# One Trainium2 kernel: the down products of the last group moved behind its gate and up products

## What is computed

```
for t in range(32):                                    # cell(h, x_t)
    r = sigmoid(x W_ih_r + h W_hh_r + b);  z = sigmoid(...)
    n = tanh(x W_ih_n + b + r * (h W_hh_n + b));  h = (1 - z) * n + z * h
gu = h @ wq_gu.T                 # 256 -> 2048, ternary weights by groups of 64
gate, up = split(gu)             # 1024 each
hid = silu(gate) * up
hn  = hid * rsqrt(mean(hid * hid) + eps)               # mean over the 1024 hidden values
out = x + hn @ wq_p.T            # 1024 -> 256
```

## Time and profile before

| | |
|---|---|
| median of 3 runs | 346.22 us (346.09 to 346.31) |
| the profiled execution | 346.3 us, of which the span of the profile is 344.5 us |
| PE busy | 339.4 us (99% of the span) |
| DVE, ACT, POOL busy | 233.6, 222.8, 184.0 us |
| granted PE clock | 1.00 of full speed |

### The profile page before, as it was taken

The page is one execution under the profiler, slowest core; times in us unless marked ns, Lnnn a source line. Parts: engine busy times, 40 slices in busy tenths (PEclk is TensorE's granted clock), DMA queues, the critical chain, the costliest instruction groups (busy, mean ns, idle before and its releaser), DMA issues.

```text
span 344.5 us, 5631 instructions
## 1 busy us (share of the span) xinstructions
PE 339.4 (99%) x2059; PEld 295.2 (86%) x2059; DVE 233.6 (68%) x462; ACT 222.8 (65%) x438; POOL 184.0 (53%) x156
## 2 busy tenths in 40 slices
PE   8999999999999999999999999999999999999996
PEld 4889988788988889888888889888888888888895
DVE  7578788899677565755667554875558555664866
ACT  5768888886756757555766656566564655756662
POOL 2315571465825446255454446444472554799694
PEclk9999999999999999999999999999999999999999
DMA  7994000045001000140001000010000100010101
GB/s 240 319 410 192 3 0 2 0 148 220 1 2 62 2 0 0 44 142 2 0 0 63 0 2 0 2 63 0 2 0 2 60 1 2 0 64 1 57 6 61
DMA packets 7891, 18.72 MB, mean 54 GB/s; under 512 B 564, under 2 KB 4788, under 8 KB 7352
## 3 DMA queue, kind: packets, MB, share of 16 engines
q1 hardware_dynamic: 7176, 17.97, 13.9%
q10 hardware_dynamic: 688, 0.39, 0.4%
HBM read 14.17 MB, written 4.19 MB: 53 GB/s over the span
## 4 chain that ended last, share of the span: by engine, by line
PE 94%; DVE 3%; ACT 1%; issue 1%; DVEq 0%
PE ps_ffn L1105 30%; PE ps_out L1143 16%; PE ps_rz L1017 7%; PE ps_rz L1022 7%; PE ps_rz L1018 7%; PE ps_n L1017 3%; PE ps_n L1022 3%; PE ps_n L1018 3%; PE ps_rz L1105 2%; PE ps_ffn L1270 2%; PE ps_t L1098 1%; PE ps_ffn L1017 1%; PE ps_ffn L1022 1%; PE ps_ffn L1018 1%; PE ps_n L1055 1%
## 5 line engine op out<-in xcount | busy, mean ns | idle before, releaser
L354 POOL TENSOR_TENSOR hid_lo<-work,hid_hi 128x512 fp32r<-128x512 f32 x62 | 81.7, 1317 | 103.6 <-ACT hid_hi L452 99.6
L1105 PE MATMUL ps_ffn<-st_hi,wguT 128*128 128x512 f32 x236 | 93.7, 397 | 0.3 <-DVE work L737 0.3
L1105 PE MATMUL ps_ffn<-st_lo,wguT 128*128 128x512 f32 x236 | 92.7, 393 | 0.0
L361 POOL TENSOR_TENSOR sq_sum<-sq_sum,work 128x512 f32<-128x512 f32 x55 | 73.2, 1331 | 1.8 <-ACT work L466 0.6
L737 DVE TENSOR_TENSOR work<-work,ps_ffn 128x512 f32<-128x512 f32 x55 | 37.6, 683 | 31.5 <-ACT work L448 31.5
L452 ACT CAST hid_hi<-work 128x512 fp32r<-128x512 f32 x63 | 38.8, 616 | 23.0 <-DVE work L747 23.0
L1105 PEld LDWEIGHTS ps_ffn<-st_hi,wguT 128*128 128x128 f32 x236 | 44.4, 188 | 8.3 <-DVE work L737 0.9
L1105 PEld LDWEIGHTS ps_ffn<-st_lo,wguT 128*128 128x128 f32 x236 | 44.5, 189 | 7.3
L747 DVE TENSOR_TENSOR work<-work,ps_ffn 128x512 f32<-128x512 f32 x63 | 43.2, 686 | 4.7 <-PE ps_ffn L1105 2.8
L1143 PEld LDWEIGHTS ps_out<-wpT,hid_hi 128*128 128x128 f32 x240 | 35.8, 189 | 3.7
L1143 PE MATMUL ps_out<-wpT,hid_lo 128*128 128x256 f32 x240 | 38.8, 284 | 0.0
(11 more groups left out here) (226 smaller groups left out, 716.0 us busy)
## 6 DMA issues: line engine op xcount, KB each, us to landing
out_dram<-o_st SPq DMA_DIRECT2D x7, 512.0 KB, 2.6
xT_all<-in_x_dram SPq DMA_DIRECT2D x1, 3072.0 KB, 17.6
x_ring<-in_x_dram SPq DMA_DIRECT2D x1, 3072.0 KB, 11.5
x_ring<-in_L_ffn_w_gate_up_dram SPq DMA_DIRECT2D x4, 512.0 KB, 8.9
x_ring<-in_L_ffn_w_proj_dram SPq DMA_DIRECT2D x2, 512.0 KB, 11.6
x_ring<-in_x_dram SPq DMA_DIRECT2D x1, 1024.0 KB, 5.4
work<-in_L_cond_W_ih_dram SPq DMA_DIRECT2D x3, 256.0 KB, 4.4
work<-in_L_cond_W_hh_dram SPq DMA_DIRECT2D x3, 256.0 KB, 4.6
```

What stands on the lines that cost most here:

```text
L354: nc.gpsimd.tensor_tensor(hid_lo[:, j % RING], hid[:, j % 2], f32(hid_hi[:, j % RING]), ALU.subtract).then_inc(hid_lo_ok, 1)
L361: nc.gpsimd.tensor_tensor(sq_sum[:], sq_sum[:], hid_sq[:, j % 2], ALU.add).then_inc(sq_added, 1)
L1105: mm = pe.matmul(bank, w, group_state(part, G, k), start=(k == 0 and i == 0), stop=(k == KD - 1 and i == 1))
```

## The change

In the last group (G = 7):

- `PE_END` now ends with all gate and up products, of tile 7 too, whole and not in halves. Down products of tiles 0 to 2 stay among them (items "E0" to "E2", in a different order of steps for tile 0). Behind "U7" come: the high parts of tiles 3 to 7, the low part of tile 3, the squares once for all eight tiles, the low parts of tiles 4 to 6, and the low part of tile 7 step by step, each step with its own signal.
- POOL computes the low parts of tiles 0 to 2 alone, and adds the squares of tiles 1 to 7. DVE computes the low parts of tiles 3 to 7: that of tile 3 behind `hidden` of tile 5, that of tile 4 behind `hidden` of tile 6, those of 5, 6 and (behind the mean) 7 at the end.
- `hid`, its high and its low parts of this group go to eight places each, in buffers that are no longer needed (`xT_all`, `wi_hi`, `wi_lo`, `wh_hi`, `wh_lo`, `hid_lo`), so `hidden` no longer waits for them. The four steps' outputs go to four banks (`ps_out` twice, `ps_n`, `ps_t`).
- The mean is made once, the power -1/2 still in two halves, and `rows_out` waits for each step's signal. The first two steps' store is now two stores.
- In all groups the square waits for `hid_ok` itself as well.

```diff
-          "U5", "D3", "G6", "U6", "D4", "Ga", "Ua", "Gb", "Ub", "D5", "H6", "T0", "T2", "Ta", "Tb", "L0", "L2"]
+          "U5", "G6", "U6", "G7", "U7"]
...
+        def hid_of(G, j):
+            return late[:, j] if is_late(G) else hid[:, j % 2]
...
+        last_out = (ps_out[:, 0, :], ps_out[:, 2, :], ps_n[:, 0:D], ps_t[:, 0:D])
+        last_sq = gate_bank(NG - 1, HT - 2)[:, 0:GS]
+        POOL_LOWS, DVE_LOWS = (0, 1, 2), (3, 4, 5, 6, 7)
...
+            for j in range(1, HT):
+                if j in POOL_LOWS:
+                    low_part(G, j)
+                add_square(G, j)
+            pool.wait_ge(ms_ok, NG)
...
-            hidden_hi(G, 5)
-            silu_part(G, 6)
-            hidden_square(G, 5)
-            hidden_hi(G, 6)
-            last_silu("a")
-            hidden_square(G, 6)
-            last_silu("b")
-            last_hi("a")
-            last_square("a")
-            last_square("b")
-            last_hi("b")
+            hidden_square(G, HT - 1)
+            hidden_hi(G, HT - 1)
...
+                for j in range(3, HT):
                     gated(G, j)
                     hidden(G, j)
+                    if is_late(G) and j in (HT - 3, HT - 2):
+                        low_part(G, j - 2)
...
+            low_part(NG - 1, 5)
+            low_part(NG - 1, 6)
+            mean_square(NG - 1)
+            low_part(NG - 1, 7)
             rows_out(NG - 1)
...
+            for j in range(3, HT):
+                late_down(hi_of, j)
+            late_down(lo_of, 3)
+            token_squares(NG - 1)
+            for j in range(4, HT - 1):
+                late_down(lo_of, j)
+            for s in range(GS):
+                late_down(lo_of, HT - 1, (s,)).then_inc(down, 1)
```

More of the change, by code:

```diff
@@ L287, in _ @@
                     sp.dma_start(x_ring[:, 0:T - XR, :], x[:, XR:T, :]).then_inc(ld_x, 16)
[L288 to L291 removed]
+            for s in range(GS - 1):
+                sp.wait_ge(o_last, s + 1)
+                sp.dma_start(out[:, T - GS + s, :], o_st[:, s, :]).then_inc(stored, 16)
+            sp.wait_ge(stored, 16 * (NG + 3))
         @block.gpsimd
@@ L651, in _ @@
                 hidden_parts(G, 1)
-                for j in range(3, HT if G < NG - 1 else HT - 2):
+                for j in range(3, HT):
                     silu_part(G, j)
@@ L1196, in down_part, with late_down @@
-            def down_part(part, ok, j, steps):
-                if j == HT - 1 and part is hid_lo:
-                    pe.wait_ge(lo_last, 1 if steps[0] == 0 else 2)
+            def late_down(part, j, steps=range(GS)):
+                G = NG - 1
+                if part is hi_of:
+                    pe.wait_ge(hid_hi_ok, 8 * G + j + 1)
                 else:
-                    pe.wait_ge(ok, 8 * (NG - 1) + j + 1 + (j == HT - 1 and steps[0] > 0))
+                    pe.wait_ge(hid_lo_ok if j in POOL_LOWS else lo_last, low_number(j))
@@ L1201, in down_part @@
                 for s in steps:
-                    mm = pe.matmul(ps_out[:, s, :], part[:, j % RING, s * P:(s + 1) * P], wpT[:, j, :],
-                                   start=False, stop=part is hid_lo and j == HT - 1, skip_group_check=True)
-                return mm
-            def last_high():
-                for first in (0, 2):
-                    down_part(hid_hi, hid_hi_ok, HT - 2, (first, first + 1))
-            def last_rows(s):
-                steps = (s, s + 1)
-                down_part(hid_hi, hid_hi_ok, HT - 1, steps)
-                down_part(hid_lo, hid_lo_ok, HT - 2, steps)
-                down_part(hid_lo, hid_lo_ok, HT - 1, steps).then_inc(down, 1)
@@ L1218, in last_squares @@
-            def last_squares(part):
-                steps = (0, 1) if part in ("0", "a") else (2, 3)
-                first = part in ("0", "2")
-                if part == "0":
-                    pe.wait_ge(ms_ok, NG - 1)
-                    pe.wait_ge(sq_added, 7 * NG - 1)
-                elif part == "2":
-                    pe.wait_ge(hid_ok, HT * NG - 1)
-                else:
-                    pe.wait_ge(sq_last, 1 if part == "a" else 2)
-                squares = sq_sum[:] if first else hid_sq[:, 1]
-                for s in steps:
-                    mm = pe.matmul(last_sq[s // 2][:, s % 2:s % 2 + 1], squares[:, s * P:(s + 1) * P], ones[:],
-                                   start=first and s % 2 == 0, stop=not first, skip_group_check=True)
-                if not first:
-                    mm.then_inc(sq_tok, 1)
+                    if j == 0 and s < 2 and part is hi_of:
+                        if s:
+                            pe.wait_ge(o_ok, G)
+                        else:
+                            pe.wait_ge(rows_read, 2)
@@ L1237, in q_group_sums @@
+                    mm = pe.matmul(last_out[s], part(G, j)[:, s * P:(s + 1) * P], wpT[:, j, :],
+                                   start=j == 0 and part is hi_of, stop=False, skip_group_check=True)
+                return mm
             def q_group_sums(u, halves=(0, 1)):
@@ L1247, in ffn_item @@
                 kind, which = item[0], item[1:]
[L1248 to L1256 removed]
+                if kind == "G":
                     gate_product(G, int(which))
@@ L1259, in ffn_item @@
                     up_product(G, int(which))
+                elif kind == "E":
+                    pe.wait_ge(ms_ok, G)
+                    steps = (2, 3, 0, 1) if which == "0" else range(GS)
+                    late_down(hi_of, int(which), steps)
+                    late_down(lo_of, int(which), steps)
                 elif kind == "D":
```

148 lines of the change are left out of this document (43 added, 105 removed).

## The result

The changed kernel takes 347.85 us (median of 7 runs, 347.60 to 349.12); before takes 346.31 beside it (346.09 to 346.62). The ratio is 1.0048, 95% interval 1.0037 to 1.0058: 1.66 us slower by the ratio (1.3 to 2.0), 1.54 by the medians. The forecast was a median of 347.6, a range of 346.4 to 348.2, and slower with 76%.

A forecast was written before the change was run, and what follows sets the result against it. PE, busy 99% of the span, was taken as the bound. PE's own work -1.0, rows nearer PE's end +0.3, waits and restarts +2.1 gave +1.4: median 347.6 us, range 346.4 to 348.2.

The forecast's parts named there:

- low part of tile 3, length: On DVE, asked for at 331.88 during POOL's addition of tile 4; ends at 333.48, 0.55 us behind that addition.
- PE resumes at the high part of tile 7: After the high parts of tiles 3 to 6, PE stands 1.7 us and resumes at 337.88.
- the holding: DVE low parts and POOL additions block each other; low parts of tiles 3, 5, 6 take 1.1 to 1.6 us, not 0.69.
- The short wait before the squares, 0.2: PE, after the low part of tile 3, waits 0.2 us for POOL's last addition, from 338.92 to 339.12.
- Squares, -0.9: On PE in the last group, 8 squares matmuls instead of 16, saving 0.9 us.
- The second wait on each square, taken at 0: On ACT in all groups, the square's added wait costs between 0 and 0.06 us; 0 taken.
- The powers, taken as not held: POOL's two powers, beside DVE's low part of tile 7, hardly held: 0.75 us each, done before the rows want them.
- The -0.2 for small things around tile 7's halves: In PE's own work, small things around tile 7's halves save 0.2 us.
- The clock, 1%: Rival: PE's 1.7 us wait could halve its clock, so 5 us of matmuls behind it cost twice; chance 1%.
- The sum: For the end of the kernel: PE's work -1.0, rows +0.3, waits and restarts +2.1, together +1.4, by the chain +1.42.
- down products behind everything cannot pay: Rival in e5's expectation: down products behind all gate and up products bring no gain, rows at 15.5 or later; no chance given.
- The first rival: PE never waits after the last up product, so the rows start 0.65 us earlier, 345.6 us; chance 8%.

The follow-up runs named there:

- e1: The changed kernel with POOL's additions of the squares of tiles 4 and 5 of the last group on 8 columns instead of 512; ratio to before 1.0022.
- e4: e2 with all five DVE low parts of the last group subtracting a PSUM bank instead of the high part in SBUF; ratio to before 1.0012.
- e2: The changed kernel with DVE's low parts of tiles 3 and 4 moved behind `hidden` of tile 7; ratio to before 1.0036.
- e10: The changed kernel with the last group's squares matmuls run twice and six filler matmuls in PE's wait for tile 7's high part; ratio to before 1.0090.
- e11: e9 with the last group's squares matmuls run twice (16 instead of 8); ratio to before 1.0016.
- e5: The changed kernel with five edits to POOL's and DVE's low parts, tile 7's square addition and PE's order; ratio to before 1.0006.
- e6: e3 with DVE's low part of tile 7 ahead of the mean instead of behind it; ratio to before 1.0046.
- e3: The changed kernel with PE taking the low parts of tiles 3 and 4 ahead of the high part of tile 7; ratio to before 1.0038.
- e12: The changed kernel, squares once, with six filler matmuls in PE's wait for the high part of tile 7; ratio to before 1.0049.
- e7: e5 with the down products of tiles 3 and 4 again between gate and up products; ratio to before 1.0067.
- e9: e5 with DVE, not POOL, adding the square of tile 6 too; ratio to before 0.9993.

## Why the prediction was right, step by step

Times from the first down matmul of tile 0, as forecast (324.91 taken off) and as measured (324.74 taken off):

| step | forecast | measured |
|---|---|---|
| gate product of tile 5 starts | 3.89 | 3.92 |
| last up product ends | 9.41 | 9.40 |
| low part of tile 3, length | 1.60 | 1.60 |
| `hidden` of tile 7 ends | 11.75 | 11.84 |
| PE resumes at the high part of tile 7 | 12.97 | 13.12 |
| POOL's last addition ends | 14.15 | 14.15 |
| squares start | 14.21 | 14.20 |
| first row out starts | 16.91 | 17.05 |

- **The place and the cause.** PE stood for 1.65 us at the high part of tile 7. That counts from the modelled end of the matmul before; counted as the forecast counts, from where the next matmul would have started (336.05), it is 1.81 against 1.68. e1 and e4 show the holding, e1 at tile 3 and e4 for all of them: with nothing changed but POOL's length or DVE's second input, the long instructions are gone and 0.75 and 0.56 us with them. Of PE's 1.65 us, 0.93 went with the holding at tile 3 (e1), and 0.53 is there without any low part ahead of `gated` (e2, e4). The Trainium skill's rule of the shared port (SBUF — State Buffer, "Who interferes with whom") agrees with the meetings of DVE's low parts with POOL's additions and powers shown above; the low part of tile 4, which began 0.04 us before POOL's end, was not held (0.68 us).
- **The short wait before the squares, 0.2.** It wasn't there: the squares start 0.14 us behind the matmul before, where 0.12 is the usual distance. PE came 0.15 us late, POOL's last addition ended on time, because its end is set by the low part of tile 5 (1.14 us behind it, 1.16 forecast) and not by its start; so it took 1.51 us and not 1.7. The two misses of PE's waits, +0.13 and -0.2, nearly cancel, which is luck.
- **Squares, -0.9.** 0.91 in e10 and 0.74 in e11.
- **The second wait on each square, taken at 0.** It is not nothing where it binds. In the chain of waits of the changed kernel there is an instruction of ACT's queue at 336.61, and the square starts 0.09 behind `hidden` (336.58 to 336.67), where ACT's high part of tile 6, with one wait, started 0.03 behind it: 0.06 us, the upper end I had put.
- **The powers, taken as not held.** Wrong. The two took 1.75 us, the first 1.08, against 0.70 each in e5 and e6, where no low part ran beside them, and in e4, where it took one input from PSUM. I had read the 0.82 us of the first power before as "hardly held". Its end says otherwise: 340.20, 0.58 behind the end of L796 (339.62); in the changed kernel it ended 0.57 behind the low part's end. It was held there too, by a shorter instruction. In the changed kernel nothing waited for it, by some 0.2 us: it ended at 341.35, and the rows, which start 0.24 behind the power where they wait for it (e5), could have started at 341.59. That the miss cost nothing is luck; in e3 it took part of the gain away.
- **The last 0.14 us.** 0.10 of it: DVE started the rows 0.14 behind the first complete step (341.65 to 341.79; the same 0.14 in e1, e4, e11 and e12), where I had taken 0.04 from before. The other 0.04 is on PE, which completed that step at 16.91 instead of 16.87.
- **Terms without a row of their own.** The -0.2 for small things around tile 7's halves is read from no row; the chain doesn't need it. The 0.69 us of a free low part came from L814, a bf16 instruction of another shape; e1 shows it for the low part itself.
- **The clock, 1%.** Too low. The profiled execution kept it until PE had nothing more to do, but of the seven executions two had a mean clock of 0.995 and took 348.6 and 349.1, the other five 347.6 to 347.9. That the clock cost them that time isn't shown: e12 has 348.63 at 0.998, and in e6 the three executions at 0.991 to 0.993 took 347.28 to 348.60, the two at full clock 347.56 and 347.95.
- **Before or after.** The sum gave +1.42, the stretch shows +1.56 and the runs +1.66 (1.3 to 2.0); the rest may come from those two executions, and lies inside the interval.

The rival "down products behind everything cannot pay" wasn't on the prediction's list but in the expectation of e5. e7 speaks against it within e5's arrangement; against the kernel before no run shows a gain clear of noise. The first rival, that PE never waits, is what e9 comes to when low parts, additions and orders are mended together, with 0.34 us of gain in the stretch and not the 0.65 that the prediction put on it.

## What to carry to other kernels

When PE's work is moved to the end to lie beside the last steps of the other engines, work out when each of its operands is ready, one by one, and put those first that are ready first; a wait for the last one in front of the queue gives the gain away. Even mended, the order here came only level with before (e5, e9). An elementwise instruction of 128x512 f32 with two SBUF inputs on VectorE did not take 0.7 us here while a GpSimd instruction that reads SBUF ran: it took what was left of GpSimd's instruction and 0.55 more, and behind it GpSimd waited in turn. Look for the end of a held instruction, not its length: an end that stands at a fixed distance behind the other engine's end is a holding even where little time was lost.
